# One block in ten transposed by VectorE instead of TensorE in the first pass, with seven read slots and another schedule of stores

## The chip, the cores and the metric

The kernel runs on one core of a Trainium2 chip. The metric is the time of one execution on the device, in microseconds (us); the median over several executions counts. A profile of one more execution goes with it.

## The reference, cut to what matters

Four graph layers with a layer norm and a residual sum after each work on `x` (5120 x 64) and one dense matrix `adj` (5120 x 5120, float32, 105 MB). What costs time are the products with `adj` and its transpose:

```python
h = adj @ (adj.T @ e)                      # layer 0, e made from x with small weights
Ax = A @ x                                 # layer 1
deg = clip(sum(adj, axis=1) + 1, 1, None)  # layer 2: row sums of adj
h_neigh = (adj @ X + X) / deg
Tx_prev1 = L_scaled @ x                    # layer 3: adj three times, one after another
for k in range(2, K):                      # K = 4
    Tx_curr = 2.0 * (L_scaled @ Tx_prev1) - Tx_prev2
x = _layernorm(x + layer(x, adj, ...))     # after each layer
```

All of it is float32.

## The kernel before, in words

`adj` is cut into 10 x 10 blocks of 512 x 512 (1 MB each, `NB = 10`, `BLOCKS = 100`). TensorE contracts over partitions, so `adj.T @ e` takes the blocks as they lie in memory and every `adj @ v` takes them transposed. The kernel has a first pass that reads each block once, and six sweeps behind it that use the transposed blocks, stored by the first pass in a DRAM tensor `at_dram`.

**The first pass** goes through the blocks column by column, n = 10 j + i, two blocks (a pair p, n = 2p and 2p + 1) at a time. The change is in this pass. For a block n:

- SyncE (SP) loads it into one of `NAT = 6` read slots (L364). The slot of block n is n mod 6, so the load of n first waits until block n - 6 has been read by all three of its readers: the transposition (`turned`), the product with `e` (`u_added`) and the row sum (`nat_summed`), L361 to L363. SP issues its loads in the order of n, so a load that waits holds all later ones.
- TensorE (PE) multiplies it with `e` (`u_part`, L549) and transposes it in 16 pieces of 128 x 128 into four PSUM banks (`turn_block`, L537).
- ScalarE (ACT) copies the four banks into one of `RING = 12` slots of `blk` (L459) and issues the store of a finished block to `at_dram` (`store`, L446). Stores are issued late by `LATE = 8` blocks in the first column, by one block less in each later column.
- VectorE (DVE) sums its rows (`sum_rows`, L793).
- Ten blocks later, when the column's vector `u` is complete, PE multiplies the transposed block with it (`h_part`, L566), and DVE adds the result to `part` (`add_h`, L777). `ps_h` has two banks: `h_part(n)` waits for the addition of n - 2.

The order on PE in a pair p from 5 on is written out by hand: `u_part(2p)`, `u_part(2p+1)`, at a column's first pair (p = 5, 10, ..., 45) `u_turn_back`, then `turn_block(2p)`, `turn_block(2p+1)`, `h_part(2p-10)`, `h_part(2p-9)`. On DVE it is `sum_rows(2p)`, `sum_rows(2p+1)`, at a column's first pair `copy_u_rows`, at its last pair `copy_u`, then `add_h(2p-10)`, `add_h(2p-9)`, and from p = 15 to 24 a small `double_x`. A column is five pairs.

When the pass ends, PE goes on with `last_h_part` (L714) and a chain over ten row blocks (L730, with `add_last_h`, L1008, and `end_l0` on DVE). The sweeps then run over `at_dram` through all 16 slots of 1 MB, with SP's loads at L387 in an order that a planner in the program works out; their first loads wait for the slots that the pass leaves (L384 to L386).

Of the kernel before, what the change touches and what calls it, by code (L numbers as in the profile page):

```python
# [29 lines left out]
ACT = mybir.ActivationFunctionType  # L30
AX = mybir.AxisListType

P = 128
# [4 lines left out]
def build(nc, x, adj, w_u, diag_u, par_u, w_i, diag_i, par_i, gamma, beta, l2_w, l2_b, l3_w, l3_b, out):  # L38
    N, F = x.shape
    BLK = 512  # L40
    NB = N // BLK
    TB = BLK // P
# [9 lines left out]
    REACH = 12  # L52
    HOLD, HELD = (3, 5), 3
    HT = TB // 2
    RING, NAT, NAT_FAR = 12, 6, 2
    SLOTS = 16
    BLOCKS = NB * NB
    COLUMN = NB // 2
    LATE = 8
    assert NB % 2 == 0 and RING >= NB + 2 and RING + NAT - NAT_FAR == SLOTS  # L60


# [6 lines left out]
    with ctx:  # L69
# [6 lines left out]
        def sem(name):  # L76
            return ctx.enter_context(nc.semaphore(name))


        blk = sb("blk", [P, SLOTS, TB, BLK])  # L80
# [41 lines left out]
        ps_t = [pb(f"ps_turn{k}") for k in range(TB)]  # L122
# [38 lines left out]
        nat_loaded = [sem(f"nat_loaded{k}") for k in range(NAT)]  # L161
        nat_summed = sem("nat_summed")
# [2 lines left out]
        u_back = sem("u_back")  # L165
        u_ready = sem("u_ready")
        turned = sem("turned")
        at_evacuated = sem("at_evacuated")
        at_stored = [sem(f"at_stored{k}") for k in range(RING)]
        multiplied = sem("multiplied")  # L170
# [132 lines left out]
        def nat(n):  # L303

            return nat_far[:, n % NAT - (NAT - NAT_FAR)] if nat_slot(n) is None else blk[:, nat_slot(n)]

        left_turned = {n % RING: n for n in range(BLOCKS - RING, BLOCKS)}
        left_nat = {nat_slot(n): n for n in range(BLOCKS - NAT, BLOCKS) if nat_slot(n) is not None}

# [42 lines left out]

        @block.sync
        def _(sp):
            for n in range(BLOCKS):
                j, i = divmod(n, NB)
                if j == 0:
                    tiles = slice(i * TB, (i + 1) * TB)
                    sp.dma_start(rows[:, tiles, :], x_rows[:, tiles, :]).then_inc(x_loaded[i], 16)
                if n >= NAT:  # L360
                    sp.wait_ge(turned, TB * (n - NAT + 1))  # L361
                    sp.wait_ge(u_added, n - NAT + 1)
                    sp.wait_ge(nat_summed, n - NAT + 1)  # L363
                sp.dma_start(nat(n), a_blocks[:, i * TB:(i + 1) * TB, j * BLK:(j + 1) * BLK])\  # L364
                    .then_inc(nat_loaded[n % NAT], 16)

            n_there = [0] * RING

            def wait_stored(n):

                if n_there[n % RING] < n // RING + 1:
                    n_there[n % RING] = n // RING + 1
                    sp.wait_ge(at_stored[n % RING], 16 * n_there[n % RING])

            for (i, j), slot, b in loads:
                wait_stored(NB * j + i)
                if slot < RING:
                    wait_stored(left_turned[slot])
                if b >= 0:
                    sp.wait_ge(block_done, b + 1)  # L380
                elif slot < RING:
                    sp.wait_ge(multiplied, left_turned[slot] + 1)
                else:
                    sp.wait_ge(turned, TB * (left_nat[slot] + 1))  # L384
                    sp.wait_ge(u_added, left_nat[slot] + 1)
                    sp.wait_ge(nat_summed, left_nat[slot] + 1)  # L386
                sp.dma_start(raw(slot).rearrange("p t n -> p (t n)"), at_dram[i, j])\  # L387
                    .then_inc(raw_loaded[slot], 16)
            for r in range(NB):
                sp.wait_ge(out_ready, r + 1)  # L390
                i = at(SWEEPS - 1, r)
                sp.dma_start(out_rows[:, i * TB:(i + 1) * TB, :], rows[:, i * TB:(i + 1) * TB, :])\
                    .then_inc(stored, 16)
            sp.wait_ge(stored, 16 * NB)
# [14 lines left out]
        def _(act):  # L409
# [26 lines left out]
            def load_turn_weights():  # L436
                for h in range(2):
                    const(twice[half(h), 0, :], l2_w[F:2 * F, :], weights_loaded)
                    const(twice[half(h), 1, :], l3_w[3], weights_loaded)
                    for k in range(2):  # L440
                        const(wide[half(h), k, 1, :], l3_w[k + 1], weights_loaded)

            def store(n):
                j, i = divmod(n, NB)
                act.wait_ge(at_evacuated, TB * (n + 1))
                act.dma_start(at_dram[i, j], blk[:, n % RING].rearrange("p t n -> p (t n)"))\  # L446
                    .then_inc(at_stored[n % RING], 16)

            def n_stored(n):

                return max(0, n + 1 - max(0, LATE - n // NB))

            for n in range(BLOCKS):
                if n >= RING:
                    act.wait_ge(multiplied, n - RING + 1)
                    act.wait_ge(at_stored[n % RING], 16 * (n // RING))
                for t in range(TB):
                    act.wait_ge(turned, TB * n + t + 1)
                    nc.scalar.activation(blk[:, n % RING, t, :], ps_t[t][:, :], ACT.Copy)\  # L459
                        .then_inc(at_evacuated, 1)  # L460
                    if t == 0 and n % 2 == 1:
                        for k in range(n_stored(n - 2), n_stored(n)):
                            if k < n:
                                store(k)
                if n % 2 == 1 and n_stored(n) == n + 1:
                    store(n)
                if n == NB + 1:
                    load_rows_of_l0()
                if n == NB + 5:
                    load_x_weights()  # L470
                if n == NB + 9:
                    load_turn_weights()

            def keep_own(b, s, r):

# [26 lines left out]
        def _(pe):  # L502
# [28 lines left out]
            def turn_block(n):  # L531
                pe.wait_ge(nat_loaded[n % NAT], 16 * (n // NAT + 1))
                for t in range(TB):
                    if n > 0:
                        pe.wait_ge(at_evacuated, TB * (n - 1) + t + 1)
                    for c in range(TB):
                        mm = pe.transpose(ps_t[t][:, c * P:(c + 1) * P], nat(n)[:, c, t * P:(t + 1) * P],  # L537
                                          ident[:, :])
                    mm.then_inc(turned, 1)
# [19 lines left out]

            def h_part(n):  # L560
                pe.wait_ge(u_ready, n // NB + 1)
                pe.wait_ge(at_evacuated, TB * (n + 1))
                if n > 1:
                    pe.wait_ge(h_added, n - 1)
                for t in range(TB):
                    mm = pe.matmul(ps_h[n % 2][half(t), :], u_rows[:, t, :], blk[:, n % RING, t, :],  # L566
                                   start=t < 2, stop=t >= TB - 2)
                mm.then_inc(multiplied, 1)
# [21 lines left out]
            for p in range(COLUMN, BLOCKS // 2):  # L590
                u_part(2 * p)
                u_part(2 * p + 1)
                if p % COLUMN == 0:
                    u_turn_back(p // COLUMN - 1)
                turn_block(2 * p)
                turn_block(2 * p + 1)
                if p == BLOCKS // 2 - 1:
                    u_turn_back(NB - 1)
                h_part(2 * p - NB)
                h_part(2 * p + 1 - NB)  # L600
# [105 lines left out]
            def last_h_part(e):  # L706
# [6 lines left out]
                for t in range(TB):  # L713
# [5 lines left out]

            row_0 = [[b for b in range(len(blocks)) if blocks[b][0] == 0 and blocks[b][1] == r]  # L720
                     for r in range(NB - 2)]
            pe.wait_ge(at_evacuated, TB * BLOCKS)
            last_h_part(0)
            for e in range(NB):
                i = NB - 1 - e
# [19 lines left out]
        def _(dve):  # L745
            V = nc.vector
# [7 lines left out]
            def copy_x_in(i):  # L754
                dve.wait_ge(xt_ready, i + 1)
                if i > 1:
                    dve.wait_ge(xw_ready, i - 1)
                V.tensor_copy(x_in_turned[i % 2], ps_h[i % 2][:, 0:HT * P]).then_inc(xt_copied, 1)
# [36 lines left out]
            def double_x(i):  # L795
# [4 lines left out]
                                       in1=vec[:, 1, :].unsqueeze(1).broadcast_to([P, TB, F]),  # L800
                                       op0=ALU.mult, op1=ALU.add)

            copy_x_in(0)
            dve.wait_ge(par_loaded, 32)
            V.tensor_tensor(par_prod[:, :], par[:, :, 0], par[:, :, 1], ALU.mult)
# [19 lines left out]
            for p in range(COLUMN, BLOCKS // 2):  # L825
                sum_rows(2 * p)
                sum_rows(2 * p + 1)
                if p % COLUMN == 0:
                    copy_u_rows(p // COLUMN - 1)
                if p % COLUMN == COLUMN - 1:  # L830
                    copy_u(p // COLUMN)
                if p == BLOCKS // 2 - 1:
                    copy_u_rows(NB - 1)
                add_h(2 * p - NB)
                add_h(2 * p + 1 - NB)
                if 0 <= p - 3 * COLUMN < NB:
                    double_x(p - 3 * COLUMN)
            dve.drain()
# [283 lines left out]
```

## Time and profile before

| | |
|---|---|
| median of 3 runs | 1528.04 us (1527.78 to 1531.92) |
| the profiled execution's own time | 1526.59 us |
| span of its instructions | 1524.7 us, which leaves 1.9 us around it |
| mean granted TensorE clock | 0.995 |
| instructions | 17451 |
| the first pass | from the start to about 544 us |

The times in the rows are of the profiled execution, from the start of its span. An engine's busy time is the time in which it has an instruction under way; matmuls overlap in the pipeline, so the start-to-start times of TensorE's groups tell more than their durations. A name with a q behind it (SPq, ACTq) is an engine's queue: it issues a DMA or waits. "To landing" is from the issue of a DMA to the last increment of its semaphore.

### The profile page before, as it was taken

To read this page: it belongs to the slowest core of one execution; us is meant where nothing else is said; L and a number is where in the kernel's file an instruction comes from. 1 tells how busy PE (TensorE), PEld (TensorE's weight loads), DVE (VectorE), ACT (ScalarE), POOL (GpSimd) and SP (SyncE) were. 2 spreads that over 40 slices of the span, in tenths; PEclk is the share of its full clock that TensorE was granted. 3 is DMA by queue.
4 is the path that set the end of the run, shared out by engine and by line. 5 is a ranking of instruction groups with operands and counts; after the bars stand their busy time and mean duration, and the time that the engine had idled before them with its cause. 6 is when DMAs were issued, how large, how long until landed. Compare 5 with 4: busy or idle time off the path is not lost.

```text
span 1524.7 us, 17451 instructions
## 1 busy us (share of the span) xinstructions
PE 1494.4 (98%) x6574; PEld 699.0 (46%) x6574; DVE 610.5 (40%) x1333; ACT 251.2 (16%) x492; POOL 61.3 (4%) x66
## 2 busy tenths in 40 slices
PE   8999999999999999999999899999999999999998
PEld 6555555555555533334444344444444444444332
DVE  5655565555556477433332544233111021110442
ACT  3333333434343310000100001000000000000000
POOL 0000000000000012100000110010000000000010
PEclk9999999999999999999999999999999999999999
DMA  9899999999999989999887487886388869988997
GB/s 310 323 395 409 411 410 413 411 409 412 413 408 411 353 328 405 421 422 389 304 315 284 156 333 302 292 297 237 131 328 312 304 223 350 336 311 301 365 421 261
DMA packets 122434, 519.09 MB, mean 340 GB/s; under 512 B 21068, under 2 KB 21108, under 8 KB 72308
## 3 DMA queue, kind: packets, MB, share of 16 engines
q1 hardware_dynamic: 105264, 412.64, 72.2%
q10 hardware_dynamic: 17092, 105.38, 16.6%
q8 instruction: 53, 0.87, 0.2%
q14 instruction: 25, 0.20, 0.0%
HBM read 411.82 MB, written 106.17 MB: 340 GB/s over the span
## 4 chain that ended last, share of the span: by engine, by line
issue 99%; POOLq 0%; POOL 0%; DVE 0%
POOL power_out L405 0%; POOLq L403 0%; POOLq L405 0%; DVE rows L881 0%; POOL ident L398 0%; POOLq L400 0%; POOL ident L400 0%; POOLq L1112 0%
## 5 line engine op out<-in xcount | busy, mean ns | idle before, releaser
L703 PE MATMUL ps_u<-blk,vectors 128*128 128x512 f32 (+1 forms) x2000 | 736.5, 595 | 1.1 <-DMA blk<-a_transposed 1.1
L703 PEld LDWEIGHTS ps_u<-blk,vectors 128*128 128x128 f32 (+1 forms) x2000 | 296.5, 173 | 394.2 <-issue 389.2
L459 ACT ACTIVATE blk<-ps_turn 128x512 f32<-128x512 f32 x400 | 205.8, 605 | 326.7 <-PE ps_turn L537 323.7
L1046 DVE TENSOR_TENSOR part<-part,ps_u 64x512 f32<-64x512 f32 (+1 forms) x45 | 30.8, 686 | 344.7 <-PE ps_u L703 343.9
L566 PE MATMUL ps_h<-blk,u_rows 128*64 128x512 f32 x720 | 164.4, 598 | 0.0
L793 DVE TENSOR_REDUCE row_part<-blk 128x4 f32<-128x2048 f32 x68 | 152.4, 2279 | 0.4
L537 PE MATMUL ps_turn<-ident,blk 128*128 128x128 f32 x1088 | 128.3, 276 | 3.6 <-DMA blk<-in_adj 3.6
L537 PEld LDWEIGHTS ps_turn<-ident,blk 128*128 128x128 f32 x1088 | 120.0, 142 | 24.1 <-issue 19.5
L777 DVE TENSOR_TENSOR part<-part,ps_h 128x512 f32<-128x512 f32 x80 | 55.0, 688 | 185.6 <-PE ps_h L566 185.6
L549 PE MATMUL ps_u<-blk,e 128*64 128x512 f32 x544 | 123.6, 594 | 0.8 <-DMA blk<-in_adj 0.8
L405 POOL TENSOR_TENSOR power_out<-power_in,minus_half 128x4 f32<-128x4 f32 x60 | 60.6, 1010 | 1459.7 <-DVEq L844 1459.7
L703 PE MATMUL ps_h<-blk,vectors 128*64 128x512 f32 x416 | 99.6, 614 | 5.0 <-issue 5.0
L481 ACT ACTIVATE part<-ps_h 64x512 f32<-64x512 f32 (+1 forms) x40 | 23.7, 593 | 432.2 <-PE ps_h L703 432.2
L566 PEld LDWEIGHTS ps_h<-blk,u_rows 128*64 128x64 f32 x720 | 47.7, 136 | 84.6 <-issue 84.6
L549 PEld LDWEIGHTS ps_u<-blk,e 128*64 128x64 f32 x544 | 38.3, 137 | 75.7 <-issue 73.8
L793 DVE TENSOR_REDUCE row_part<-nat_far 128x4 f32<-128x2048 f32 x32 | 71.7, 2279 | 0.1
L537 PEld LDWEIGHTS ps_turn<-ident,nat_far 128*128 128x128 f32 x512 | 55.8, 141 | 9.8 <-issue 9.7
L537 PE MATMUL ps_turn<-ident,nat_far 128*128 128x128 f32 x512 | 59.4, 274 | 0.0
L1062 DVE TENSOR_TENSOR part<-part,ps_h 64x512 f32<-64x512 f32 x28 | 19.2, 685 | 97.1 <-PE ps_h L703 96.2
L549 PE MATMUL ps_u<-nat_far,e 128*64 128x512 f32 x256 | 57.9, 593 | 0.0
L703 PEld LDWEIGHTS ps_h<-blk,vectors 128*64 128x64 f32 x416 | 28.2, 140 | 61.3 <-issue 60.1
L498 ACT ACTIVATE u_turned<-ps_turn 128x256 f32<-128x256 f32 x20 | 7.7, 383 | 288.6 <-PE ps_turn L642 288.6
(109 smaller groups left out, 610.7 us busy)
## 6 DMA issues: line engine op xcount, KB each, us to landing
blk<-a_transposed SPq DMA_DIRECT2D x291, 1024.0 KB, 5.8
a_transposed<-blk ACTq DMA_DIRECT2D x100, 1024.0 KB, 9.8
blk<-in_adj SPq DMA_DIRECT2D x68, 1024.0 KB, 22.1
nat_far<-in_adj SPq DMA_DIRECT2D x32, 1024.0 KB, 22.0
rows<-in_x SPq DMA_DIRECT2D x10, 128.0 KB, 9.3
out<-rows SPq DMA_DIRECT2D x10, 128.0 KB, 3.9
w3x<-in_L_gnn_weight ACTq DMA_DIRECT2D x6, 16.0 KB, 9.6
w2x<-in_L_gnn_W ACTq DMA_DIRECT2D x4, 16.0 KB, 9.8
```

Source lines behind the costliest of these rows:

```text
L405: nc.gpsimd.tensor_tensor(power_out[:, :], power_in[:, :], minus_half[:, :], ALU.pow)\
L459: nc.scalar.activation(blk[:, n % RING, t, :], ps_t[t][:, :], ACT.Copy)\
L481: nc.scalar.activation(part[parts, i * BLK:(i + 1) * BLK], ps_own[s == 0][r % 2][parts, :], ACT.Copy).then_inc(own_copied, 1)
L498: nc.scalar.activation(u_turned[:, 0:HT * P], ps_xt[:, 0:HT * P], ACT.Copy)\
L537: mm = pe.transpose(ps_t[t][:, c * P:(c + 1) * P], nat(n)[:, c, t * P:(t + 1) * P], ident[:, :])
L549: mm = pe.matmul(ps_u[j % 2][half(c), :], e_rows[:, i * TB + c, :], nat(n)[:, c, :], start=i == 0 and c < 2, stop=i == NB - 1 and c >= TB - 2)
L566: mm = pe.matmul(ps_h[n % 2][half(t), :], u_rows[:, t, :], blk[:, n % RING, t, :], start=t < 2, stop=t >= TB - 2)
L703: mm = pe.matmul(acc, left, tiles[:, t, :], start=first, stop=last)
L777: V.tensor_tensor(part[:, cols], part[:, cols], ps_h[n % 2][:, :], ALU.add)\
L793: V.reduce_sum(row_part[:, i * TB:(i + 1) * TB, j], nat(n), AX.X).then_inc(nat_summed, 1)
L1046: V.tensor_tensor(part[parts, cols], part[parts, cols], ps_both[r % 2][parts, :], ALU.add)\
L1062: V.tensor_tensor(part[parts, cols], part[parts, cols], ps_own[0][r % 2][parts, :], ALU.add)\
```

## The change

Block 4 of each column but the first (n = 14, 24, ..., 94: nine blocks, `BY_DVE`) is no longer transposed by PE and copied by ACT. DVE transposes it, in 16 instructions that each move 32 partitions x 512 elements from quadrant a of the read slot to quadrant b of the slot of the ring, as sixteen 32 x 32 blocks. They are dealt over three pairs: pieces 0 to 4 at the end of DVE's work for the block's own pair n // 2, pieces 5 to 10 a pair later, pieces 11 to 15 two pairs later. The semaphore `turned_by_dve` is raised behind piece 15. It takes the place of `turned` and `at_evacuated` for these blocks: for the load that reuses the slot, for the store, for `h_part`, and for PE ahead of `last_h_part(0)`.

There are 7 read slots in place of 6 (three of them, before two, outside `blk`), so the load of n waits for block n - 7. A store is due `max(LATE - n // 10, 2)` blocks late with `LATE = 6`, a block turned by DVE at least 6 late, and what is due after the last block is issued after the loop.

```diff
-    RING, NAT, NAT_FAR = 12, 6, 2
+    RING, NAT, NAT_FAR = 12, 7, 3
+    BY_DVE = list(range(NB + 4, BLOCKS, NB))
+    Q = P // 4
-    LATE = 8
+    LATE = 6
...
+        def by_pe(n):
+            return sum(k not in BY_DVE for k in range(n + 1))
...
+            def wait_read(n):
+                sp.wait_ge(turned, TB * by_pe(n))
+                if n in BY_DVE:
+                    sp.wait_ge(turned_by_dve, BY_DVE.index(n) + 1)
+                sp.wait_ge(u_added, n + 1)
+                sp.wait_ge(nat_summed, n + 1)
...
                 if n >= NAT:
-                    sp.wait_ge(turned, TB * (n - NAT + 1))
-                    sp.wait_ge(u_added, n - NAT + 1)
-                    sp.wait_ge(nat_summed, n - NAT + 1)
+                    wait_read(n - NAT)
...
-            def n_stored(n):
-                return max(0, n + 1 - max(0, LATE - n // NB))
+            def stored_at(n):
+                return n + max(LATE - n // NB, 6 if n in BY_DVE else 2)
...
+            for n in range(BLOCKS):
+                if stored_at(n) >= BLOCKS:
+                    store(n)
...
             def h_part(n):
                 pe.wait_ge(u_ready, n // NB + 1)
-                pe.wait_ge(at_evacuated, TB * (n + 1))
+                if n in BY_DVE:
+                    pe.wait_ge(turned_by_dve, BY_DVE.index(n) + 1)
+                else:
+                    pe.wait_ge(at_evacuated, TB * by_pe(n))
...
-                turn_block(2 * p)
-                turn_block(2 * p + 1)
+                for n in (2 * p, 2 * p + 1):
+                    if n not in BY_DVE:
+                        turn_block(n)
...
-            pe.wait_ge(at_evacuated, TB * BLOCKS)
+            pe.wait_ge(at_evacuated, TB * by_pe(BLOCKS - 1))
+            pe.wait_ge(turned_by_dve, len(BY_DVE))
             last_h_part(0)
...
+            def turn_some(n, pieces):
+                slot = n % RING
+                if 0 in pieces:
+                    dve.wait_ge(nat_loaded[n % NAT], 16 * (n // NAT + 1))
+                    if n >= RING:
+                        dve.wait_ge(multiplied, n - RING + 1)
+                        dve.wait_ge(at_stored[slot], 16 * (n // RING))
+                for k in pieces:
+                    a, b = divmod(k, 4)
+                    tiles_in = nat(n)[a * Q:(a + 1) * Q, :, :].rearrange("p c (t b q) -> p b c t q", t=TB, b=4)[:, b]
+                    tiles_out = blk[b * Q:(b + 1) * Q, slot].rearrange("p t (c a q) -> p a c t q", c=TB, a=4)[:, a]
+                    V.transpose(tiles_out, tiles_in)
+                if 15 in pieces:
+                    dve.drain().then_inc(turned_by_dve, 1)
...
                 add_h(2 * p - NB)
                 add_h(2 * p + 1 - NB)
+                for n in BY_DVE:
+                    if 0 <= p - n // 2 < 3:
+                        turn_some(n, (range(5), range(5, 11), range(11, 16))[p - n // 2])
```

## Rows read from the trace of the kernel before

**Rows 1.** The page: TensorE's and VectorE's busy time, DMA share by 40 slices.

```profile
PE 1494.4 (98%) x6574; PEld 699.0 (46%) x6574; DVE 610.5 (40%) x1333; ACT 251.2 (16%) x492; POOL 61.3 (4%) x66
...
DMA  9899999999999989999887487886388869988997
```

**Rows 2.** A window of 40 us in the first pass.

```profile
core 0: us, PE busy (x) PEld busy (x) DVE busy (x) ACT busy (x) POOL busy (x), PEclk, DMA share, GB/s
280.00:320.00 40.00, 40.00 (x240) 20.92 (x240) 20.79 (x17) 15.96 (x32) 0.00 (x0) 1.00 1.03 412
```

**Rows 3.** Timeline of one pair (p = 27): start, length, engine, work.

```profile
299.82 3.71 PE L537 MATMUL ps_turn<-ident,blk 128*128 128x128 f32 x32
...
301.82 17.83 SPq L364 DMA_DIRECT2D blk<-in_adj  x4
...
303.46 3.65 PE L566 MATMUL ps_h<-blk,u_rows 128*64 128x512 f32 x16
...
306.95 3.60 PE L549 MATMUL ps_u<-blk,e 128*64 128x512 f32 x16
...
307.17 0.69 DVE L777 TENSOR_TENSOR part<-part,ps_h 128x512 f32<-128x512 f32 x1 [1.03 <-PE ps_h L566]
...
307.77 4.47 DVE L793 TENSOR_REDUCE row_part<-blk 128x4 f32<-128x2048 f32 x2
...
310.48 3.71 PE L537 MATMUL ps_turn<-ident,blk 128*128 128x128 f32 x32
```

**Rows 4.** Timeline of PE at two columns' first pairs (p = 25, 30).

```profile
274.41 3.60 PE L549 MATMUL ps_u<-blk,e 128*64 128x512 f32 x16
277.94 0.66 PE L557 MATMUL ps_u<-ident,u_turned 128*128 128x128 f32 x4
...
328.27 3.60 PE L549 MATMUL ps_u<-blk,e 128*64 128x512 f32 x16
```

**Rows 5.** PE's waits before 640 us: total, times, longest.

```profile
PE ps_turn L537 <- DMA blk<-in_adj: 3.6, 1, 3.6
...
PE ps_u L549 <- DMA blk<-in_adj: 0.8, 1, 0.8
```

**Rows 6.** L364, loads issued at 39 to 53, 1 to 2, 56 to 60, 100 to 540 us.

```profile
DMA to landing us min/median/max: 5.1/5.4/5.8
...
DMA to landing us min/median/max: 8.0/8.0/8.0
...
DMA to landing us min/median/max: 8.7/9.1/9.5
...
DMA to landing us min/median/max: 15.3/22.3/27.8
```

**Rows 7.** DVE's groups of instructions by shape: busy us, mean ns of one.

```profile
L793 DVE TENSOR_REDUCE row_part<-blk 128x4 f32<-128x2048 f32 x68 | 152.4, 2279 | 0.4
...
L777 DVE TENSOR_TENSOR part<-part,ps_h 128x512 f32<-128x512 f32 x80 | 55.0, 688 | 185.6 <-PE ps_h L566 185.6
...
L881 DVE TENSOR_TENSOR vectors<-temp,power_out 128x256 f32<-128x256 f32 x30 | 12.8, 425 | 12.9 <-POOL power_out L405 12.0
...
L783 DVE COPY u_turned<-ps_u 128x512 f32<-128x512 f32 x10 | 6.8, 683 | 1.6 <-PE ps_u L549 1.6
```

**Rows 8.** Windows around two idle times of PE in the sweeps (columns as in rows 2).

```profile
1441.80:1444.50 2.70, 0.02 (x2) 0.00 (x0) 1.79 (x5) 0.00 (x0) 1.01 (x1) 0.95 1.00 422
1444.50:1447.60 3.10, 3.08 (x10) 1.48 (x12) 2.63 (x12) 0.00 (x0) 0.43 (x1) 0.50 1.01 423
...
872.10:877.60 5.50, 5.48 (x14) 1.91 (x16) 4.16 (x21) 0.60 (x1) 1.01 (x1) 0.50 0.16 25
```

**Rows 9.** Timeline where the first pass ends.

```profile
543.79 1.89 PE L714 MATMUL ps_h<-blk,x_close 128*64 128x512 f32 x8
...
545.73 0.69 DVE L1008 TENSOR_TENSOR part<-part,ps_h 128x512 f32<-128x512 f32 x1 [1.03 <-PE ps_h L714]
...
546.50 0.66 PE L730 MATMUL ps_turn<-ident,part 128*128 128x128 f32 x4 [0.82 <-DVEq L1009]
```

More of the change, by code:

```diff
@@ L167, in build @@
         turned = sem("turned")
+        turned_by_dve = sem("turned_by_dve")
         at_evacuated = sem("at_evacuated")
@@ L383, in _ @@
                 else:
-                    sp.wait_ge(turned, TB * (left_nat[slot] + 1))
-                    sp.wait_ge(u_added, left_nat[slot] + 1)
-                    sp.wait_ge(nat_summed, left_nat[slot] + 1)
+                    wait_read(left_nat[slot])
                 sp.dma_start(raw(slot).rearrange("p t n -> p (t n)"), at_dram[i, j])\
@@ L444, in store @@
                 j, i = divmod(n, NB)
-                act.wait_ge(at_evacuated, TB * (n + 1))
+                act.wait_ge(at_evacuated, TB * by_pe(n))
+                if n in BY_DVE:
+                    act.wait_ge(turned_by_dve, BY_DVE.index(n) + 1)
                 act.dma_start(at_dram[i, j], blk[:, n % RING].rearrange("p t n -> p (t n)"))\
                     .then_inc(at_stored[n % RING], 16)
-            def n_stored(n):
-                return max(0, n + 1 - max(0, LATE - n // NB))
+            def stored_at(n):
+                return n + max(LATE - n // NB, 6 if n in BY_DVE else 2)
             for n in range(BLOCKS):
-                if n >= RING:
+                if n >= RING and n not in BY_DVE:
                     act.wait_ge(multiplied, n - RING + 1)
@@ L457, in _ @@
                 for t in range(TB):
-                    act.wait_ge(turned, TB * n + t + 1)
-                    nc.scalar.activation(blk[:, n % RING, t, :], ps_t[t][:, :], ACT.Copy)\
-                        .then_inc(at_evacuated, 1)
+                    if n not in BY_DVE:
+                        act.wait_ge(turned, TB * (by_pe(n) - 1) + t + 1)
+                        nc.scalar.activation(blk[:, n % RING, t, :], ps_t[t][:, :], ACT.Copy)\
+                            .then_inc(at_evacuated, 1)
                     if t == 0 and n % 2 == 1:
-                        for k in range(n_stored(n - 2), n_stored(n)):
-                            if k < n:
+                        for k in range(n):
+                            if n - 2 < stored_at(k) <= n:
                                 store(k)
-                if n % 2 == 1 and n_stored(n) == n + 1:
+                if n % 2 == 1 and stored_at(n) <= n:
                     store(n)
@@ L534, in turn_block @@
                     if n > 0:
-                        pe.wait_ge(at_evacuated, TB * (n - 1) + t + 1)
+                        pe.wait_ge(at_evacuated, TB * (by_pe(n) - 2) + t + 1)
                     for c in range(TB):
@@ L561, in h_part @@
                 pe.wait_ge(u_ready, n // NB + 1)
-                pe.wait_ge(at_evacuated, TB * (n + 1))
+                if n in BY_DVE:
+                    pe.wait_ge(turned_by_dve, BY_DVE.index(n) + 1)
+                else:
+                    pe.wait_ge(at_evacuated, TB * by_pe(n))
                 if n > 1:
@@ L594, in _ @@
                     u_turn_back(p // COLUMN - 1)
-                turn_block(2 * p)
-                turn_block(2 * p + 1)
+                for n in (2 * p, 2 * p + 1):
+                    if n not in BY_DVE:
+                        turn_block(n)
                 if p == BLOCKS // 2 - 1:
```

## Prediction

> **What bounds the kernel now.** I read the page first: TensorE (PE) has work under way in 98% of the span, every other engine in 40% or less, and the DMA engines in most slices nine tenths [rows 1]. A busy PE is not yet a PE at its peak, so three views of the first pass follow. In a window in its middle PE is busy for 40.00 of 40 us at the full granted clock, DVE for 20.8, ACT for 16.0, and the DMA engines move 412 GB/s at a share of 1.03 [rows 2]. The timeline of one pair gives PE's real pace by its starts: two blocks transposed in 303.46 - 299.82 = 3.64 us, `h_part` twice in 3.49, `u_part` twice in 3.53, together 10.66 us from one turn to the next [rows 3]. A column is five such pairs and the turning back of `u`: 328.27 - 274.41 = 53.9 us = 5 x 10.66 + 0.6 [rows 4]. And PE's waits in the pass are 3.6 us for the very first block and 0.8 us once later, both for a load [rows 5]. So PE sets the end of the pass, and what is taken from PE there shortens it one for one, as long as no load comes late. Loads are near that point: they take 22.3 us from issue to landing in the steady state [rows 6], while six slots are 3 pairs = 32 us of PE's time, and a slot is only given back at the end of the turn phase of its pair, 3.49 + 2 x 10.66 = 24.8 us ahead of its next use. Two or three microseconds are the whole margin.
>
> **The change, part by part.** E is the moment at which PE finishes a column's last pair (p = 9 for the first gate), which is also the start of the next `u_part`, 306.95 in [rows 3].
>
> *Transposes taken from PE.* 16 of them take 3.64 / 2 = 1.82 us [rows 3]. Nine blocks: 16.4 us gained at the most, 1.1% of the time. The four ACT copies a block that fall away are hidden, since ACT is idle for over half of the window [rows 2].
>
> *Where the sixteen DVE pieces end.* The last five stand behind `add_h(9)` in DVE's order, and that addition waits for `h_part(9)`, the last thing PE does in pair 9. So block 14 is never fully turned before E. The addition starts 0.22 us after E and takes 0.69: 0.91 us [rows 3]. Then come five transposes. The trace has none on DVE. The nearest rows by elements per partition are operations of 512 elements, 0.683 to 0.688 us; below them stands the 256-element one with 0.425; above them, if a 4-byte word went at half the rate, 0.688 + 512 x (2.279 - 0.688) / 1536 = 1.22 us [rows 7]. I take 0.69, an element a cycle as in all these rows, and keep 0.43 and 1.22 as ends. Five make 3.45 us.
>
> The Trainium skill, Vector Engine (DVE) Microarchitecture Reference, section on the reshape front-end, says that the transposing array is pipelined to sustain one element per cycle per lane; no run so far shows it, and its sum would be the same 3.45. Its page VectorE: DVE Perf Modes, section on two Vector instructions with no wait between them, says that an instruction whose output starts in another quadrant than the last one's starts only when all before it have finished. Every piece here does that. The trace shows neighbours that overlap by 2 x 2.279 - 4.47 = 0.09 us [rows 3, 7]; with that overlap five pieces would take 3.0 us, by the rule the full 3.45.
>
> *What waits for piece 15.* Loads: the load of block n reuses the slot of n - 7, and 14 + 7 = 21. So the loads of blocks 21, 31, ..., 91, eight of them, wait for `turned_by_dve`, and SP holds every later load behind them. Block 21 is the second block of pair 10, the very pair that PE begins at E. PE can do `u_part(20)`, 3.53 / 2 = 1.77 us, and then has nothing: `u_part(21)` needs the block, and its transposes and `h_part(10)`, `h_part(11)` stand behind it in PE's order. The slot before was free after PE's own transposes, some 25 us ahead of use; now it is free 0.91 + 3.45 = 4.4 us *after* the pair has begun. The seventh slot moves the load that is held from n = 20 to n = 21 and gives one more `u_part` of cover; it does not reach over three pairs of DVE pieces.
>
> *The stall, per column.* From E: addition 0.91; five pieces 3.45; drain to release 546.50 - (545.73 + 0.69) = 0.08 us [rows 9]; release to SP's issue 301.82 - (299.82 + 1.82) = 0.18 us [rows 3]; landing. All earlier loads have landed long before and the loads behind are held, so the load meets a queue with at most two stores in it. Loads issued so took 5.1 to 5.8 us, the first load of the kernel, with small loads ahead and others behind it, 8.0, loads with two stores issued just ahead 8.7 to 9.5 [rows 6]. I take 6.0, with ends 5.1 and 9.1. The sum less PE's cover: 0.91 + 3.45 + 0.26 + 6.0 - 1.77 = 8.9 us of idle PE.
>
> *The clock behind it.* After 2.7 us without work PE ran at 0.50 of its clock (1.2 GHz) for the next 3.1 us of work; elsewhere for 5.5 us [rows 8]. Work at half the clock takes twice the time, so such a stall costs 1.55 to 2.75 us more; I take 2.15. An idle time of 8.9 us is longer than these, so I expect it each time.
>
> *Whether DVE keeps up.* Between E of pair 8 and E of pair 9 DVE has six pieces, two sums 4.47, `copy_u` 0.68 and two additions 1.38 [rows 3, 7]: 6 x 0.69 + 6.53 = 10.67 against PE's 10.66. It just fits; each 0.1 us more for a piece puts 0.6 us on the lag and 0.5 on the last five, 1.1 us a column. `h_part` needs only additions of a pair earlier, so such a lag acts through the gate alone. `h_part(10)` needs `copy_u_rows`, behind `sum_rows(21)`, 2.3 us after block 21 lands; PE then has 1.77 and 3.64 us of other work, so no second stall.
>
> *After the gate.* Six loads go out at once, and PE wants them two per 10.66 us; the mean need of a column, 21 MB in some 63 us, is far below 412 GB/s [rows 2]. Nothing.
>
> *Stores.* Fewer blocks late means 6 early stores instead of 8 held back and three stores (94, 98, 99) behind the loop. Their bytes are the same and lie beside PE work; the stalls leave the DMA engines idle anyway. Zero, up to 2 us at the end of the pass if they hold the sweeps' first loads.
>
> *The end of the pass.* `last_h_part(0)` waits for block 94: 0.91 + 3.45 + 0.08 = 4.4 us after PE's last `h_part`, where PE went on at once at 543.79 [rows 9]. Behind it PE waits for DVE's chain at times, so of the low clock I count 1 us.
>
> **Sum.** Eight columns x (8.9 + 2.15 - 1.82 = 9.2) = 73.8; block 94's own transposes -1.8; end of the pass 4.4 + 1 = 5.4; together +77.4. The profiled execution took 1526.59 us, so 1604.0; the median of the runs stands 1.45 above it, so **1605 us**, 5% slower.
>
> **The rivals.**
> - *The load is in time and the change does what it takes away from PE.* All nine transposes gained, 1528.0 - 16.4 = 1512 us. For it: PE is the bound [rows 1, 2, 5]. It decides from the point where piece 15 ends one landing, 6 us on an idle queue and 22 on a full one, ahead of `u_part(21)`; by the order above it ends 4.4 - 1.8 = 2.6 us behind the moment at which PE wants the block. 3%; no change by a balance of both, 1%.
> - *DVE's transposes are the slower ones,* 1.22 us. The last five take 6.1, and DVE falls behind by (5 x 1.22 + 5.85) - 10.66 = 1.3 and (6 x 1.22 + 6.53) - 10.66 = 3.2 us in the pairs before. The stall becomes 8.9 + 2.65 + 4.5 = 16.0, a column 16.4, the end 12.5: 8 x 16.4 - 1.8 + 12.5 = +142, 1670 us. For it: no row of such an instruction. 10%.
> - *The DMA engines don't catch up:* six loads and the stores share the rings, block 21 lands with the burst. At 9.1 us a column costs 3.1 more, 1630 us, still in the forecast's range; at the 22.3 of the steady state 16 more, some 1735. Against it: the first load landed in 8.0 with others behind it [rows 6]. 5% beyond the range.
> - *The stall is small:* pieces of 0.43, landing in 5.1, and the clock stays. 8 x (8.9 - 1.3 - 0.9 - 1.82) = 39, less 1.8 and plus 3.1: 1568 us. 4%.
>
> **How the numbers follow.** The forecast has the rest, 77%. Its range: low, pieces at 0.6, landing 5.1, clock 1.55, no clock at the end: 1605 - 8 x (0.45 + 0.9 + 0.6) - 1.5 = 1588, and some for two of the bounds at once, 1580. High, landing 9.1 (+25), clock 2.75 (+5), and pieces a tenth slower (+6): 1641. With what of the rivals falls inside, 1580 to 1642 holds 8 in 10. A difference of 0.3% is about what a measurement of this kernel can tell. Faster 3%, within it 1%, slower 96%.
>
> **What the profile after would show.** A wait of PE at the `u_part` line on a load from `adj`, eight times, 8 to 10 us each, at a column's second block; transposes on DVE of 0.69 us, 144 of them; SP's queue waiting for DVE at the load line; half the granted clock for some microseconds behind each wait; columns of 63 us in place of 53.9, pairs with the DVE block of 8.8 us; a wait of 4 us ahead of L714's counterpart. The sweeps behind the pass unchanged to 2 us. The prediction is wrong if block 21 is found landed when PE comes to it, and off in size if the pieces, the landing or the clock lie elsewhere.

## The result and the profile after

The changed kernel takes 1612.99 us (median of 4 runs, 1611.18 to 1615.69) against 1527.91 of the kernel before beside it: a ratio of 1.056 with a 95% interval of 1.054 to 1.058, so 85 us slower. The forecast was 1605 us within 1580 to 1642, slower at 96%.

The page of the changed kernel, to be held against [rows 1]:

```profile
span 1612.4 us, 17288 instructions
...
PE 1506.7 (93%) x6430; PEld 690.4 (43%) x6430; DVE 714.0 (44%) x1477; ACT 233.8 (14%) x456; POOL 61.3 (4%) x66
...
PEclk9999898899999997999999999999999999999999
DMA  9979699798797796999978848887458887888997
```

TensorE has gone from 98% to 93% of a longer span. In the first 16 slices, the first pass, the granted clock and the DMA share have dips that [rows 1] lacks; behind them the DMA digits are much as they were. The place of the loss is the pass: from its start to the first L730 (L753 now) it took 546.50 us before and takes 632.30, 85.8 more, of 87.7 in all. The sweeps, in a window of 960 us of each kernel, hold the same work: PE 945.88 us busy and 313 GB/s before (556 to 1516 us), 946.45 and 317 after (640 to 1600).

PE's waits before 640 us, the view of [rows 5] (total, times, longest), and, in the second block, SP's over the span:

```profile
PE ps_u L567 <- DMA blk<-in_adj: 44.9, 7, 8.2
PE ps_u L567 <- DMA nat_far<-in_adj: 25.8, 4, 8.2
PE ps_h L736 <- DVEq L840: 4.6, 1, 4.6
...
PE ps_u L575 <- DVE u_turned L806: 3.1, 1, 3.1
```

```profile
SPq L368 <- DVEq L840: 251.8, 8, 38.8
...
SPq L377 <- PE ps_turn L555: 116.4, 35, 8.4
...
SPq L367 <- DVEq L840: 36.9, 1, 36.9
```

Where PE waited 0.8 us for a load after the first block, it waits 70.7 us in 11 places, all at `u_part` (L567). L840 is the drain that raises `turned_by_dve`, and L364 to L368 are the waits in front of a load. SP, the queue of the loads, stood there for 251.8 + 36.9 us until `turned_by_dve` was raised, some 32 us a time in nine places (the ninth, for block 94's slot, stands among the sweeps' first loads). That is the wait that the change adds.

One of the eight places, the first pair of the column of blocks 60 to 69, in the timeline:

```profile
365.73 3.65 PE L587 MATMUL ps_h<-blk,u_rows 128*64 128x512 f32 x16
...
368.78 1.34 DVE L800 TENSOR_TENSOR part<-part,ps_h 128x512 f32<-128x512 f32 x2
369.21 1.89 PE L567 MATMUL ps_u<-nat_far,e 128*64 128x512 f32 x8
370.15 3.58 DVE L838 STREAM_TRANSPOSE blk<-nat_far 32x512 f32<-32x512 f32 x5
373.83 0.92 SPq L377 DMA_DIRECT2D nat_far<-in_adj  x2
...
379.07 3.68 PE L567 MATMUL ps_u<-nat_far,e 128*64 128x512 f32 x8 [7.97 <-DMA nat_far<-in_adj]
```

This is the chain of the forecast, link by link: `h_part` ends, DVE adds, turns five pieces, SP issues at 373.83, the load lands 5.2 us later, and PE, done with `u_part(60)` after 1.9 us, has been idle for 7.97. The product of one block, 1.89 us before the gap, takes 3.68 behind it: the clock.

Windows of the same column (columns as in [rows 2]), from the gap on:

```profile
370.80:379.10 8.30, 0.33 (x4) 0.03 (x2) 5.21 (x7) 0.00 (x0) 0.00 (x0) 0.83 0.50 166
379.10:383.10 4.00, 4.00 (x10) 1.16 (x11) 2.24 (x1) 0.00 (x0) 0.00 (x0) 0.50 1.05 390
383.10:420.00 36.90, 36.90 (x226) 20.04 (x226) 22.18 (x19) 14.46 (x28) 0.00 (x0) 1.00 1.03 411
420.00:435.90 15.90, 13.21 (x76) 6.26 (x72) 14.76 (x17) 4.13 (x8) 0.00 (x0) 1.00 0.45 183
```

Read the last two numbers of each row. Behind the gap PE works 4.0 us at 0.50 of its clock, which costs 2. For 41 us the DMA engines are full (411 GB/s at 1.03, as in [rows 2]). Then, with SP held again, they are at 0.45 for the 16 us up to the next gate, as they were at 0.50 in the gap that the first row shows. (A gate is the moment at which DVE's last piece lets the held load go.) Over the stretch from 100 to 540 us their share is 0.86 after and 1.02 before. This the forecast did not weigh, and the experiments turned on it.

### The profile page after: what moved, and what is told of

It is laid out like the page before. It is cut to its first block, busy times and chain, and to the rows that moved or that the text cites. A ratio compares the mean times of both kernels' runs of the same rounds, so it can differ in the third digit from the quotient of the medians.

```text
span 1612.4 us, 17288 instructions
## 1 busy us (share of the span) xinstructions
PE 1506.7 (93%) x6430; PEld 690.4 (43%) x6430; DVE 714.0 (44%) x1477; ACT 233.8 (14%) x456; POOL 61.3 (4%) x66
## 3 DMA queue, kind: packets, MB, share of 16 engines
q1 hardware_dynamic: 105264, 412.64, 68.4%
## 4 chain that ended last, share of the span: by engine, by line
issue 99%; POOLq 0%; POOL 0%; DVE 0%
POOL power_out L416 0%; POOLq L414 0%; POOLq L416 0%; DVE rows L923 0%; POOL ident L409 0%; POOLq L411 0%; POOL ident L411 0%; POOLq L1154 0%
## 5 line engine op out<-in xcount | busy, mean ns | idle before, releaser
L473 ACT ACTIVATE blk<-ps_turn 128x512 f32<-128x512 f32 x364 | 188.4, 608 | 416.8 <-PE ps_turn L555 415.3
L567 PE MATMUL ps_u<-blk,e 128*64 128x512 f32 x464 | 116.9, 640 | 44.9 <-DMA blk<-in_adj 44.9
L816 DVE TENSOR_REDUCE row_part<-blk 128x4 f32<-128x2048 f32 x58 | 130.9, 2282 | 14.5 <-DMA blk<-in_adj 13.8
L567 PE MATMUL ps_u<-nat_far,e 128*64 128x512 f32 x336 | 82.8, 626 | 25.8 <-DMA nat_far<-in_adj 25.8
L555 PE MATMUL ps_turn<-ident,blk 128*128 128x128 f32 x832 | 101.7, 280 | 3.6 <-DMA blk<-in_adj 3.6
L555 PEld LDWEIGHTS ps_turn<-ident,blk 128*128 128x128 f32 x832 | 94.6, 145 | 21.2 <-issue 17.0
L816 DVE TENSOR_REDUCE row_part<-nat_far 128x4 f32<-128x2048 f32 x42 | 94.9, 2282 | 9.1 <-DMA nat_far<-in_adj 8.5
L567 PEld LDWEIGHTS ps_u<-blk,e 128*64 128x64 f32 x464 | 33.8, 145 | 114.4 <-issue 63.2
L555 PEld LDWEIGHTS ps_turn<-ident,nat_far 128*128 128x128 f32 x624 | 68.5, 142 | 13.1 <-issue 13.0
L555 PE MATMUL ps_turn<-ident,nat_far 128*128 128x128 f32 x624 | 74.0, 275 | 0.0
L838 DVE STREAM_TRANSPOSE blk<-blk 32x512 f32<-32x512 f32 x96 | 67.4, 702 | 1.4
L567 PEld LDWEIGHTS ps_u<-nat_far,e 128*64 128x64 f32 x336 | 24.4, 143 | 75.7 <-issue 46.3
```

What stands on the lines that cost most here:

```text
L567: mm = pe.matmul(ps_u[j % 2][half(c), :], e_rows[:, i * TB + c, :], nat(n)[:, c, :], start=i == 0 and c < 2, stop=i == NB - 1 and c >= TB - 2)
L816: V.reduce_sum(row_part[:, i * TB:(i + 1) * TB, j], nat(n), AX.X).then_inc(nat_summed, 1)
L838: V.transpose(tiles_out, tiles_in)
```

## The experiments

All times are medians, each ratio is to the kernel before beside it on the same chip. Each diff is against the changed kernel and shows its main lines. Sums of waits and of low clock are of the profiled executions and are held against their spans.

**The slots and the schedule of stores alone.** All blocks back on TensorE; seven slots and the new schedule stay.

```diff
-    BY_DVE = list(range(NB + 4, BLOCKS, NB))
+    BY_DVE = []
...
-            pe.wait_ge(turned_by_dve, len(BY_DVE))
```

> All blocks are transposed by TensorE again; the seventh read slot and the new schedule of stores stay. If the whole loss comes from the loads that wait for VectorE's last piece, this runs as the kernel before: 1528 us within 4 us, without a wait of PE for a load after the first block. If the slots or the schedule of stores have a part in it (a fuller or emptier DMA queue at the wrong time), it stays above 1535 us, and waits at the u_part line are seen.

Measured: 1525.03 us, ratio 0.9986 (0.9976 to 0.9995). PE does not wait for a load in the pass after the first block. So these two parts of the change are harmless together, if anything worth 2 us, and the whole loss hangs on `BY_DVE`: 88 us.

**The wait alone.** No block is turned by DVE; the eight loads wait for the addition that ends the column.

```diff
-    BY_DVE = list(range(NB + 4, BLOCKS, NB))
+    BY_DVE = []
...
                     wait_read(n - NAT)
+                if n > 2 * NB and n % NB == 1:
+                    sp.wait_ge(h_added, n - NB - 1)
```

> All blocks transposed by TensorE, no work for VectorE added; only the loads of blocks 21, 31, ..., 91 wait in addition for VectorE's addition that ends a column (the one in front of pieces 11 to 15 in the changed kernel). The wait without the work: the stall is 0.91 + 0.26 + 5.1 - 1.77 = 4.5 us eight times and its low clock 1.5 to 2.5 us, so 1525 + 8 x 6.5 = 1577 us (1570 to 1585). If the loss came from VectorE's work and not from the held loads, it stays near 1525.

Measured: 1585.62 us, 1.038 (1.036 to 1.040), 61 us over the run above, 9 over the middle of the expectation and just above its range. PE's waits of the profiled execution:

```profile
PE ps_u L569 <- DMA blk<-in_adj: 22.6, 5, 5.1
PE ps_u L569 <- DMA nat_far<-in_adj: 14.5, 3, 6.0
```

Eight waits, 37.1 us, 4.6 each as worked out. The rest is the clock: it stayed low for 2.8 to 5.8 us of work behind each, 36 us in all, so 18 us where 12 to 20 were expected. The held load, without one instruction of transposing on DVE, makes two thirds of the loss. The rest follows by a sum and not by a run: 61, and 8 x 3.6 for the pieces in the gate, and 12.5 for the end of the pass (below), less 16.4 for PE's relief, are some 85 of the 88 us.

**PE kept busy through the gap.** 68 transposes of the identity (work without use) between the two `u_part` of a gate.

```diff
                 u_part(2 * p)
+                if p % COLUMN == 0 and p > COLUMN:
+                    pe.wait_ge(at_evacuated, TB * by_pe(2 * p - 1))
+                    for k in range(FILL):
+                        pe.transpose(ps_t[TB - 1][:, k % TB * P:(k % TB + 1) * P], ident[:, :], ident[:, :])
                 u_part(2 * p + 1)
```

> The changed kernel with 68 transposes of the identity into a free PSUM bank between u_part of the first and the second block of columns 2 to 9 (added work without use; 68 x 0.114 = 7.75 us at the full clock, just under the stall of 7.8 to 8.2). They delay nothing that the load doesn't delay, but PE is not idle. If the low clock behind each stall comes from the idle time and costs half of its length on work (30 us of work at 0.50 behind the eight gates, so 15 us), the time falls by 12 to 17 us to 1596 to 1601. If the clock does not matter (the loads would hold PE again anyway), it stays at 1613 within 3 us.

Measured: 1621.85 us, 1.062 (1.060 to 1.064): 9 us slower, a miss for both theories. The gate itself went as planned (the timeline, then PE's waits in the pass):

```profile
377.54 7.65 PE L617 MATMUL ps_turn<-ident 128*128 128x128 f32 x68
385.45 1.94 PE L568 MATMUL ps_u<-nat_far,e 128*64 128x512 f32 x8 [0.26 <-DMA nat_far<-in_adj]
```

```profile
PE ps_u L568 <- DMA blk<-in_adj: 14.2, 9, 5.6
PE ps_u L568 <- DMA nat_far<-in_adj: 12.0, 7, 5.6
```

`u_part` behind the filling takes 1.94 us, not 3.68: no low clock there. Of the 16 places eight are the gates themselves, 3.1 us. In the other eight PE waits 23.1 us for later loads, up to 5.6 us at once, where the changed kernel waits 6.8 in three places, and behind six of the eight the clock falls after all. The column from 375.72 to 438.03 took 62.3 us, the same column in the changed kernel 62.1. So the 2 us of a gate that the clock costs are not free to be won: behind PE stands the DMA queue, which has six held loads and the stores to catch up with. The columns of blocks 30 to 39 and 40 to 49 took 68.4 us each against 63.2 and 64.6, and in each PE waits 5.6 us for a later load against 1.1 and 1.6. The two are 9.0 us longer together. In the second of them three stores go out 15.0 to 15.8 us after its start instead of 17.5 to 18.3, and the fifth to seventh load behind the gate land 19.1, 28.6 and 32.1 us after their issue instead of 15.0, 24.4 and 28.1. That the earlier stores delayed these loads fits, and no run isolates it.

**Two pairs instead of three.** The gate opens most of a pair earlier.

```diff
-                    if 0 <= p - n // 2 < 3:
-                        turn_some(n, (range(5), range(5, 11), range(11, 16))[p - n // 2])
+                    if 0 <= p - n // 2 < 2:
+                        turn_some(n, (range(8), range(8, 16))[p - n // 2])
```

> The sixteen pieces are dealt 8 and 8 over two pairs, so the block is fully turned a pair earlier: the load held by it goes out 0.91 + 8 x 0.70 + 0.26 = 6.8 us after the end of pair 8 instead of 4.6 us after that of pair 9, and lands at about 12, when PE wants it at 12.4. Theory of the serial chain (PE stalls only because addition, pieces, issue and landing follow one another behind the pair's end): the eight stalls of 8 us shrink to 0 to 1.5 us and their low clock goes, all but the transposes' gain returns, 1512 to 1526 us. Rival (the DMA engines have no time to lose: a column's 21 MB take 51 us at 412 GB/s of the 52.1 that PE leaves, and each held queue is time lost to them): PE waits for loads elsewhere in the column, several us a column, 1535 to 1570 us.

Measured: 1575.00 us, 1.030 (1.026 to 1.034). The serial chain is refuted as the only cause; the time is 5 us above the rival's 1535 to 1570. PE's waits, and the window of 100 to 540 us:

```profile
PE ps_u L567 <- DMA blk<-in_adj: 22.9, 6, 4.9
PE ps_u L567 <- DMA nat_far<-in_adj: 18.2, 5, 4.0
...
PE ps_u L575 <- DVE u_turned L806: 5.3, 1, 5.3
```

```profile
100.00:540.00 440.00, 398.91 (x2258) 202.82 (x2255) 310.96 (x295) 134.98 (x262) 0.00 (x0) 0.96 0.92 357
```

Waits of 46.4 us and 36.9 us of work at half the clock, which cost 18.5, less the 16.4 of PE's relief, are 48.5 of the 50.9 us by which this profile is longer than that of the run with all blocks on PE.

**An odd block.** The same work at the same places, but the held load is block 22's, a pair later in PE's order.

```diff
-    BY_DVE = list(range(NB + 4, BLOCKS, NB))
+    BY_DVE = list(range(NB + 5, BLOCKS, NB))
```

> Block 5 of each column instead of block 4, the pieces in the same three pairs at the same places. The load that is held is now that of block 22, the first of pair 11, and not of block 21, the second of pair 10: PE has pair 10 as cover, 10.7 us more, against a stall of 8. Serial chain: the release and the landing of the held load are where they were (landing 5.1 us after issue, about 10 us after the end of pair 9), no stall at it or at most 1 us, 1512 to 1526 us. Rival (DMA time): the queue is held as long as in the changed kernel, so waits at later loads, 1535 to 1570 us. Both: if block 94 has become 95, the wait of 4.6 us at the end of the pass stays.

Measured: 1597.29 us, 1.045 (1.041 to 1.049), above both expectations, although PE has 10.7 us more of cover. Its waits:

```profile
PE ps_u L567 <- DMA blk<-in_adj: 21.9, 9, 4.2
PE ps_h L587 <- DVE u_rows L810: 17.6, 8, 2.7
PE ps_u L567 <- DMA nat_far<-in_adj: 8.4, 4, 3.1
```

The 8 us gap at the gate is gone and 30.3 us of waits for loads are left, spread over 13 places, with a DMA share of 0.89 in the window of 100 to 540 us. What the gap had hidden comes out too: `u_rows` waits on DVE behind pieces 11 to 15 and two row sums, 2.1 to 2.7 us a column. I had said that no second stall comes from `copy_u_rows`; that held only while PE was late anyway. The time lies above both expectations by about what the clock costs: two or three short waits a column instead of one long one leave 56 us of PE's work at 0.50, which cost 28 us, where the changed kernel has 47 us of such work.

**Own slot.** The seventh slot is kept for the DVE blocks, the others go round six.

```diff
+            k = NAT - 1 if n in BY_DVE else (n - sum(m in BY_DVE for m in range(n))) % (NAT - 1)
+            place.append(k)
+            user_before.append(users[k][-1] if users[k] else None)
...
-                if n >= NAT:
-                    wait_read(n - NAT)
+                if user_before[n] is not None:
+                    wait_read(user_before[n])
```

> As the changed kernel, but the seventh read slot belongs to the blocks that VectorE turns and the other blocks go round six slots; nothing is loaded into the seventh for ten blocks, so no load waits for a piece. Both the serial chain and the rival that came out of the first runs (the DMA queue runs empty behind the held load and its time is missing later in the column) say that the cause is gone: no waits of PE at a column's second block, DMA share in the pass back at 1.0. Then PE saves 9 x 1.82 = 16.4 us from the 1525 of the kernel with all blocks on PE, and the end of the pass keeps its waits of 3.1 and 4.6 us and their low clock, some 10 us: 1517 to 1522. If the DMA engines are then the bound (21.4 MB a column at 412 GB/s are 51.9 us against 52.1 of PE), PE waits for loads here and there, up to 1525. If neither holds and DVE's transposes themselves cost PE something (shared memory ports), it stays above 1540.

Measured: 1553.00 us, 1.017 (1.015 to 1.020): 60 us of the 85 are gone, 30 more than expected are not. The time lies where the expectation puts DVE's transposes costing PE something by themselves. The waits speak for another cause: PE waits 16.2 us for `u_rows`, 7.7 at the end of the pass and 5.5 for loads, and the low clock costs 12.6, which less 16.4 is 25.6 of the 26.0 us over the profile of the run with all blocks on PE. The runs with two pairs, below, decide it.

**Own slot, block 94 left to PE.** `range(NB + 4, BLOCKS - NB, NB)` in addition.

> As the one before, with block 94 left to TensorE, so that nothing at the end of the pass waits for VectorE's pieces. Costs 1.8 us of transposes, saves the waits of 3.1 and 4.6 us and the low clock behind them, 3 us or more: 6 to 9 us below the run before, 1510 to 1515 us. If the end of the pass was hidden by the DMA-bound start of the sweeps, it is within 2 us of it.

Measured: 1542.76 us, 1.009 (1.008 to 1.011), 10 us below the run above, as expected or a little more: the end of the pass was not hidden. What is left, in PE's waits and in SP's:

```profile
PE ps_h L595 <- DVE u_rows L818: 16.1, 8, 2.7
PE ps_u L575 <- DMA blk<-in_adj: 7.0, 3, 4.3
```

```profile
SPq L376 <- DVEq L848: 104.2, 7, 16.5
```

An own slot alone does not free the queue. SP runs some six blocks ahead, so in a column's last pair it comes to the next DVE block's load and waits up to 16.5 us for the piece that ends behind that pair. And PE still waits 2 us a column for `u_rows`.

**Own slot and two pairs; own slot, two pairs and block 2.** The first keeps block 4 and leaves 94 out; the second has `range(NB + 2, BLOCKS, NB)`.

> The own slot, no block 94, and the pieces dealt 8 and 8 over two pairs. The own slot alone left a hold: SP works some six blocks ahead, so it comes to the load of block 24 in pair 9 and there waits up to 16.5 us for block 14; and PE waited 2.1 us a column for u_rows, which stands on VectorE behind pieces 11 to 15. Two pairs end both: block 14 is turned 6.8 us after the end of pair 8, where SP wants its slot at about 5 to 7, and no piece stands in a column's last pair. If these two are what is left of the loss, 1525 - 8 x 1.82 = 1510 us, up to 1516 with a wait here and there. If the DMA engines have no room for a faster PE, 1518 to 1526.

> As the one before with block 2 of each column but the first (nine blocks): the pieces lie in pairs 6 and 7 of a column's pairs 5 to 9, and VectorE has two pairs to catch up before copy_u and u_rows are wanted. Block 92 is turned well before the end of the pass. VectorE's lag theory: 1 to 3 us faster than the run before, 1508 to 1513. DMA bound: the same as the run before, 1518 to 1526.

Measured: 1524.40 us, 0.9981 (0.9971 to 0.9991), and 1519.82 us, 0.9946 (0.9929 to 0.9962). The loss is gone, with eight and nine blocks still transposed by DVE: to shorten the hold and to move the pieces from in front of `u_rows` removes all of it. The hold is shorter and not gone: SP still waits for the pieces, 39.8 us in seven places in the first and 52.6 in eight, up to 9.7 us, in the second. The gain is small. The second's waits in the pass, and the windows of two of its columns, the one of blocks 20 to 29 and the one of 60 to 69 (the last three numbers are PE's granted clock, the DMA share and GB/s):

```profile
PE ps_u L575 <- DMA nat_far<-in_adj: 3.8, 1, 3.8
PE ps_u L575 <- DMA blk<-in_adj: 2.5, 1, 2.5
```

```profile
110.30:167.90 57.60, 53.84 (x310) 27.54 (x308) 41.16 (x38) 18.59 (x36) 0.00 (x0) 0.97 1.03 406
328.40:380.40 52.00, 52.00 (x312) 27.11 (x310) 40.98 (x38) 18.59 (x36) 0.00 (x0) 1.00 1.03 404
```

Six of the columns from block 10 to block 89 take 52.0 to 52.1 us, where the kernel before took 53.7 to 53.9: in them PE has its 1.8 us whole, within 0.1, with the transposes on DVE. So the transposes themselves cost PE nothing. The gain is missing in two columns, that of blocks 20 to 29 (5.5 us of wait and low clock) and that of blocks 40 to 49 (4.2).

**No pieces.** Fifteen of the sixteen transposes of each DVE block are left out, so these blocks' transposed part is not computed: PE's relief for next to no work on DVE, and for a hold of the queue of 8.7 us at the most.

```diff
-                    if 0 <= p - n // 2 < 3:
-                        turn_some(n, (range(5), range(5, 11), range(11, 16))[p - n // 2])
+                    if p == n // 2:
+                        turn_some(n, range(15, 16))
```

> The changed kernel with 15 of the 16 pieces of each block left out (these blocks are not transposed by anyone, so their part of the result is not computed); the one that is left stands in the block's own pair and gives the slot free 1.9 us after its end. What the relief of PE is worth if it costs VectorE nothing and holds no load for long: 9 x 1.82 = 16.4 us if PE is the bound to the end, 1525 - 16 = 1509 us. If the DMA engines bound the pass as soon as PE is faster, less: 1515 to 1525.

Measured: 1520.04 us (6 runs, 1515.95 to 1524.97), 0.9957 (0.9937 to 0.9976), so 5 us below the run with all blocks on PE, of 16.4 taken from PE. The profiled execution is at the fast end (span 1514.8, 10.4 less than 1525.2). In it PE waits 4.0 us once for a load, in the column of blocks 20 to 29. The rows are the window of 100 to 520 us, this column, and that of blocks 60 to 69:

```profile
100.00:520.00 420.00, 415.98 (x2458) 216.21 (x2456) 249.10 (x193) 148.61 (x288) 0.00 (x0) 1.00 1.03 410
...
110.20:167.90 57.70, 53.72 (x310) 27.26 (x308) 31.01 (x23) 18.59 (x36) 0.00 (x0) 0.97 1.04 409
...
324.30:376.30 52.00, 52.00 (x311) 27.12 (x309) 30.81 (x23) 18.59 (x36) 0.00 (x0) 1.00 1.03 410
```

Of the 6.0 us that are missing from 16.4, the wait and the low clock behind it are 5.6. The DMA engines are full all through, and still six of the eight columns from block 10 to block 89 take 52.0 us: a share of 1.03 did not by itself bar the gain.

**Stores later.** The fastest version with `LATE = 8`, and with a floor of 4 in place of 2 as well.

> The fastest version so far (own slot, block 2, two pairs) with the stores of the early columns as late as in the kernel before: LATE = 8 in place of 6, still never under 2. That version's only waits of PE in the pass are 3.8 us at 132 us and 2.5 us at 253 us, both for a load, where the DMA engines are full (share 1.02 to 1.05) and stores take up to 334 of 420 GB/s. Two more stores put off take 2 MB, 5 us at 412 GB/s, out of that stretch. If the lack of DMA time there makes the waits, the first goes, with its low clock: 3 to 6 us faster, 1514 to 1517 us. If the waits come from the order in which the queues are served and not from the amount, no change: 1519 to 1521.

> The same with stores never under 4 blocks late, so that two more are left for the time behind the last block. The pass then has 2 MB less to move in its second half, where no wait of PE was seen; the sweeps' first loads, for which the DMA engines are the bound, come behind two more stores: 5 us of DMA time. Expected 0 to 5 us slower than the run beside it, 1515 to 1521; if the pass itself was held back by DMA time in a way that the waits don't show, up to 2 us faster.

Measured: 1521.31 us, 0.9962 (0.9949 to 0.9976), and 1519.67 us, 0.9945 (0.9927 to 0.9963): no gain over 0.9946. By the first's expectation this speaks for the order in which the queues are served and against the amount of DMA time. It does not settle it, since the waits moved: the one of 3.8 us is gone in both, and four of 1.0 to 2.1 us, 5.9 in all, stand in its place in the first and two, 3.5 in all, in the second. The version with the own slot, two pairs and block 2 takes 0.5% less time than the kernel before; it is the one to keep.

## Why the prediction was right, and where it was off

- *What takes the time.* Right, and shown by the wait alone and by the own-slot runs: the loads held by `turned_by_dve`, not DVE's transposes as such and not the slots or the stores.
- *The stall.* 8.9 us forecast, 7.8 to 8.2 measured, 63.9 in the eight. The addition ended 0.91 us after E (forecast 0.91), five pieces took 3.58 (3.45), the release some 0.1 (0.26), the load 5.0 to 5.4 (6.0). Landing was the term taken too long; it was the low end of [rows 6]. The forecast's 3.0 us for five pieces that overlap by 0.09 should have been 3.1, four overlaps and not five; nothing else used it.
- *The clock.* 2.15 forecast; behind the eight gaps PE worked 30.4 us at half the clock, 15.2 us or 1.9 each. The size was right, the term less independent than I had it: with PE kept busy the time came back as waits.
- *The eight columns and the ninth block:* 63.9 + 15.2 - 16.4 = 62.7 against 73.8 - 1.8 = 72.0 forecast.
- *After the gate: nothing.* This is the step that failed. I compared a column's mean need with the DMA engines' rate. But the loads come in a burst behind each gate, and where stores shared the engines (65% of their time from 392 to 412 us), loads issued between 383 and 400 us needed 22.8 to 28.8 us to land. In columns 2 to 4 three of them came late, 4.1, 1.1 and 1.6 us of waits and 1.7 for the clock: 8.5 us.
- *DVE just keeps up.* So it did inside the columns, 0.70 a piece. At the last pair it did not: six pieces of block 94 stand before `copy_u`, and PE turns `u` back in that same pair and not a pair later. PE waited 3.1 us there and worked 6.0 us at half the clock behind it. I had read the lag as acting through the gate alone.
- *The end of the pass.* 4.4 forecast, 4.6 measured. With the wait for `copy_u`, its clock (3.0), and 1.8 for the low clock behind the second wait, the end cost 12.5 us against 5.4.
- *The sum.* 62.7 + 8.5 + 12.5 = 83.7 of 87.7 us; about 2 us lie in the pass without a cause that I can name, and of the 2 behind it the low clock makes 1.7: it lasts until 635.7 us, over 3.4 us of work. Forecast 77.4: the gates were taken 9 us too dear, and the burst and the end 16 us too cheap.
- *The rival of the full gain.* I gave it all 16.4 us if the loads came in time. Without pieces and in the best version 5 us came out against the run with all blocks on PE, and 8 against the kernel before. In most columns the loads were in time and the gain was whole; what is missing stands in one or two early columns, each with one late load. I had the loads in time everywhere or nowhere, where it is settled column by column. Whether those loads are late for want of DMA time, by the order of the queues or by what is left of the hold is not shown.

Left open: why later loads come later in the kernel with PE kept busy, and what the slower runs without pieces, up to 1524.97 us, lose, since only a fast one was profiled.

## What to carry to other kernels

When a buffer gets a slower reader, look for the transfer that reuses it and for everything behind that transfer in the same queue, and place the last read by that transfer's due time, not by the due time of the reader's own result: here the transposed block was wanted five pairs after its own, the load into its read slot had to land by the third pair after it, and the pieces ended only when that pair had begun. Count the cover in the consumer's order of work, since one more slot can be worth a single product. Where the transfer engines are as full as the bounding engine, a held queue costs their idle time even if no one waits at the gate, as the odd block showed. What is taken from the bounding engine then pays only where no load comes late, so look at it column by column and not in the sum. Short waits are not cheap either, since many bring a stretch of low clock of their own.

## What the runs showed of the hardware

DVE's transpose of 32 partitions x 512 float32 elements took 702 ns on average over 144 (689 to 708), and five in a row took 3.58 us, so with every output in another quadrant than the last none overlapped its neighbour, where two row sums did by 0.08. The Trainium skill, VectorE: DVE Perf Modes, section on two Vector instructions with no wait between them, says that such an instruction starts only when all before it have finished; the trace agrees. A 1 MB load of 2 KB rows issued to an idle queue landed in 5.0 to 5.4 us with five loads behind it, and the next three 2.7 us apart, where the forecast had 6.0 and the kernel's first load had taken 8.0. PE's clock fell behind some waits of 2 us and not behind others: with PE kept busy, behind 2.03 us at 153 us and not behind 2.03 us at 418. A product of one block behind a gap of 8 us took 3.68 us in place of 1.89. Work on PE did not get slower beside DVE's transposes: a column took 52.0 us with 16 of them in it and with one.
